# Mamba's product of B with the input on GpSimd in place of VectorE, under a newly searched plan

## What is computed

```
xn = layernorm(x)
x  = x + mamba(xn) + experts(xn)          # L0: Mamba (256 channels, 16 states) and a top-1 mixture of 8 experts
xn = layernorm(x)
x  = x + attention(xn) + local_layers(xn) # L1: 16 heads of 8 with a distance kernel; two local-attention layers, window 64

# inside mamba, for each channel d, state n and token t:
deltaA  = exp(dt * A)                     # dt = softplus(...)
deltaBx = dt * B[t, n] * xs[t, d]
h       = deltaA * h + deltaBx            # a scan over the tokens
y[t, d] = sum over n of h * C[t, n]
```

## Time and profile before

| what | value |
| --- | --- |
| time, median of 3 runs | 2417.98 us (2406.57 to 2421.41) |
| span of the profiled execution | 2423.0 us |
| PE busy | 1912.3 us, 79% |
| DVE busy | 1905.3 us, 79% |
| ACT busy | 1819.8 us, 75% |
| POOL busy | 611.8 us, 25% |
| DMA, mean | 52 GB/s |
| chain that ended last | PE 29%, DVE 29%, issue 20%, ACT 18% |

### The profile page before, as it was taken

How to read it: one execution, slowest core, us unless ns; L and a number is a source line. 1 busy time by engine, 2 the same in 40 slices (tenths; PEclk the granted TensorE clock), 3 DMA queues, 4 the chain that set the end, 5 groups by cost and what they waited for, 6 DMA issues and landing times.

```text
span 2423.0 us, 31144 instructions
## 1 busy us (share of the span) xinstructions
PE 1912.3 (79%) x10610; PEld 1286.1 (53%) x10610; DVE 1905.3 (79%) x2685; ACT 1819.8 (75%) x2507; POOL 611.8 (25%) x270
## 2 busy tenths in 40 slices
PE   3767788898777888887787888878778787888776
PEld 2533446675545555554555555545445555556555
DVE  5878885538998799869997998878986988765563
ACT  2435778888768888787778887788778687888884
POOL 2532211222222213212232222322222222213220
PEclk9887879998879789888888888989898988997887
DMA  7731205531110120011101110101101110000000
GB/s 242 240 106 58 70 18 146 148 88 62 44 44 9 49 75 27 9 50 53 48 5 41 40 56 18 45 11 47 40 23 41 42 55 18 1 1 5 1 1 5
DMA packets 67517, 126.19 MB, mean 52 GB/s; under 512 B 8836, under 2 KB 40132, under 8 KB 67236
## 3 DMA queue, kind: packets, MB, share of 16 engines
q1 hardware_dynamic: 61808, 113.19, 14.7%
q0 software_dynamic: 2816, 7.21, 0.9%
q10 hardware_dynamic: 2740, 3.80, 0.4%
HBM read 111.33 MB, written 12.85 MB: 51 GB/s over the span
## 4 chain that ended last, share of the span: by engine, by line
PE 29%; DVE 29%; issue 20%; ACT 18%; DMA 2%; SPq 1%; DVEq 0%; ACTq 0%; another core or an unknown queue 0%
PE ps L776 6%; DVE hB L1458 6%; PE ps L968 5%; DVE hB L1464 3%; PE ps L1010 3%; DVE hB L1452 3%; PE ps L1070 3%; ACT L771 3%; ACT arena L1281 2%; ACT arena L1289 2%; DVE arena L1529 2%; DVE n_c L1537 2%; DVE lss L1583 2%; ACT arena L1355 2%; DVE rb L1590 2%
## 5 line engine op out<-in xcount | busy, mean ns | idle before, releaser
L1749 POOL TENSOR_TENSOR arena<-arena 128x1024 f32<-128x1024 f32 x128 | 359.2, 2826 | 972.5 <-ACT arena L1283 972.5
L776 PE MATMUL ps<-w_ident,arena 128*128 128x128 f32 x1647 | 276.6, 316 | 135.6 <-ACT arena L1355 42.8
L968 PE MATMUL ps<-hB,w_ident 128*128 128x512 f32 x512 | 305.6, 728 | 70.7 <-DVE hB L1464 68.8
L776 PEld LDWEIGHTS ps<-w_ident,arena 128*128 128x128 f32 x1647 | 223.8, 164 | 228.3 <-issue 113.6
L1458 DVE TENSOR_TENSOR_SCAN hB<-dA,hB 128x1024 f32<-128x1024 f32 x128 | 321.1, 2514 | 1.0 <-ACT dA L1245 0.6
L1753 POOL TENSOR_TENSOR arena<-arena,rb 128x1024 f32<-128x1024 f32 x64 | 159.2, 2487 | 622.5 <-DVE rb L1590 622.5
L1070 PE MATMUL ps<-w_l_wqkv,arena 128*128 128x512 f32 x384 | 205.3, 666 | 30.7 <-DVE rb L1590 12.5
L1245 ACT ACTIVATE dA<-mv,w_A_log 128x510 f32<-128x510 f32 x256 | 168.3, 714 | 70.9 <-DVE hB L1458 68.0
L1452 DVE TENSOR_TENSOR hB<-BC,mv 128x1024 f32<-128x1024 f32 x128 | 194.3, 1522 | 29.8 <-PE ps L968 28.1
L1529 DVE TENSOR_SCALAR arena<-ps 128x1024 f32<-128x1024 f32 x128 | 155.8, 1217 | 58.9 <-PE ps L1010 54.6
L1355 ACT ACTIVATE arena<-ps,nmx 128x128 f32<-128x128 f32 (+1 forms) x512 | 159.2, 394 | 55.6 <-DVE nmx L1610 52.7
(11 more groups left out here) (210 smaller groups left out, 4066.0 us busy)
## 6 DMA issues: line engine op xcount, KB each, us to landing
BC<-bc_d SPq DMA_DIRECT2D x128, 512.0 KB
BC<-in_experts SPq DMA_DIRECT2D x16, 514.0 KB
arena<-in_experts SPq DMA_DIRECT2D x15, 514.0 KB
mv<-in_experts SPq DMA_DIRECT2D x15, 514.0 KB, 3.4
arena<-in_x SPq DMA_DIRECT2D x8, 256.0 KB, 5.5
xnT_d<-arena SPq DMA_DIRECT2D x8, 256.0 KB, 10.9
hB<-xnT_d SPq DMA_DIRECT2D x8, 256.0 KB
x<-in_x SPq DMA_DIRECT2D x8, 256.0 KB, 2.8
```

What stands on the lines that cost most here:

```text
L776: return t.transpose(out_, in_, ident[0:k, 0:k])
L968: e = t.matmul(lb(), ident, hB[k % 2][:, j], start=q == 0 and j == 0, stop=q == NQ - 1 and j == NG - 1)
L1749: g.tensor_tensor(la[m % 2][:, half], la[m % 2][:, half], cl[:, half], ALU.subtract).then_inc(g_sub, 1)
```

## The change

`m_bx` moves from the vector program to the GpSimd program, with the same waits (the buffer's `m_sum` of two steps before, `du`, the load of B); whoever waited for `v_bx` (the scan, SP's next load of B) now waits for `g_bx`. All the planner's numbers are replaced: costs in `STAGES`, a landing time for each engine in `LANDS`, and `LATER` and `STREAM`, which were searched anew. The planner also has a new rule: units named in `DUAL` (on DVE) and in `POOLED` (on POOL) don't run at the same time in the plan, the later one waits for the earlier to end. The order on every engine changes with this.

```
 STAGES = {
-    ... "m_bx": [("DVE", 1.35)], "m_scan": [("DVE", 2.4)], "m_hc": [("DVE", 1.35)], "m_sum": [("PE", 2.3)],
+    ... "m_bx": [("POOL", 2.36)], "m_scan": [("DVE", 2.28)], "m_hc": [("DVE", 1.22)], "m_sum": [("PE", 1.72)],
...
-LANDS = {"SP": 4.5, "POOL": 2.0}
+LANDS = {"PE": 0.27, "ACT": 0.12, "DVE": 0.12, "SP": 4.5, "POOL": 0.15}
+DUAL = ("m_du", "m_scan", "m_hc", "m_fin", "qn", "g_hd")
+POOLED = ("g_sub", "qkv", "m_bx")
-LATER = {"down": 7, "e_down": 10, "e_lg": -58, ...
+LATER = {"down": -23, "e_down": 12, "e_lg": -121, ...
...
+                if e == "DVE" and unit[0] in DUAL:
+                    takes += max(0.0, pool_until - now)
+                    dual_until = now + takes
+                if e == "POOL" and unit[0] in POOLED:
+                    takes += max(0.0, dual_until - now)
+                    pool_until = now + takes
...
 vector_program:
-                elif u == "m_bx":
-                    ...
-                    v.tensor_tensor(hB[k % 2], Bb[q % 2], bc(du[:, c:c + 1], [P, NG, T]), ALU.mult).then_inc(v_bx, 1)
                 elif u == "m_scan":
-                    v.wait_ge(v_bx, m + 1)
+                    v.wait_ge(g_bx, m + 1)
 gpsimd_program:
+                elif u == "m_bx":
+                    q, c = divmod(k, CH)
+                    m = STEPS * i + k
+                    if m >= 2:
+                        g.wait_ge(p_ys, m - 1)
+                    if k < 2:
+                        g.wait_ge(v_du, CH * (i + 1))
+                        g.wait_ge(p_xp, 3 * (i + 1))
+                        g.wait_ge(d_bc, 16 * (i + 1))
+                    g.wait_ge(d_B[q % 2], 16 * ((NQ * i + q) // 2 + 1))
+                    g.tensor_tensor(hB[k % 2], Bb[q % 2], bc(du[:, c:c + 1], [P, NG, T]), ALU.mult).then_inc(g_bx, 1)
 sync_program, m_B:
-                        s.wait_ge(v_bx, CH * (m - 1))
+                        s.wait_ge(g_bx, CH * (m - 1))
```

More of the change, by code:

```diff
@@ L64 @@
[L64 to L72, removed]
-    "shift": [("PE", 0.4), ("ACT", 0.8)], "norm": [("DVE", 0.2), ("ACT", 0.5)], "qn": [("DVE", 1.25)], "heads": [("PE", 1.2), ("ACT", 0.9)],
@@ new lines @@
+    "m_ex": [("ACT", 1.34)], "m_bx": [("POOL", 2.36)], "m_scan": [("DVE", 2.28)], "m_hc": [("DVE", 1.22)], "m_sum": [("PE", 1.72)],
+    "m_fin": [("DVE", 1.47)], "x_load": [("SP", 0.1)], "m_out": [("PE", 1.8), ("DVE", 0.69)],
+    "f_yg": [("POOL", 4.8)], "f_ln": [("DVE", 2.46), ("ACT", 0.55)], "f_xn": [("DVE", 1.11)], "f_tr": [("PE", 0.44), ("DVE", 0.68)],
+    "g_qkv": [("PE", 0.65), ("DVE", 0.62)], "g_sq": [("ACT", 1.06), ("DVE", 1.54)], "g_norm": [("ACT", 0.9)],
+    "g_hd": [("DVE", 0.29), ("PE", 0.44), ("ACT", 0.59)], "g_score": [("PE", 1.06), ("DVE", 1.22)], "g_ln": [("ACT", 4.05)],
@@ L112, in stages, with lands @@
     if u == "m_in":
-        return [("PE", 1.1), ("ACT", 0.6)] if k % 2 else [("PE", 1.1), ("DVE", 2.9), ("ACT", 0.65)]
+        return [("PE", 0.86), ("ACT", 0.62)] if k % 2 else [("PE", 0.86), ("DVE", 3.15), ("ACT", 0.62)]
     if u == "e_scat":
-        return [("POOL", 1.3 * TT * (GP[n + 1] - GP[n]))]
+        return [("POOL", 1.5 * TT * (GP[n + 1] - GP[n]))]
     if u == "qkv":
-        return [("PE", 1.15), ("ACT", 0.5)] if k % 3 else [("PE", 2.3), ("ACT", 0.95), ("DVE", 3.55), ("POOL", 2.4)]
+        return [("PE", 0.86), ("ACT", 0.6)] if k % 3 else [("PE", 1.72), ("ACT", 1.02), ("DVE", 3.6), ("POOL", 2.36)]
     return STAGES[u]
+def lands(unit, engine):
+    return 2.0 if engine == "POOL" and unit[0] in ("e_scat", "f_yg") else LANDS[engine]
 def stream(unit):
@@ L454, in schedule @@
                 if best[2] and best[2] != table:
[L455 removed]
+                    takes += LOAD_TIME * (2 if best[2] == "tan" and table == "ln" else 1)
                     table = best[2]
+                if e == "DVE" and unit[0] in DUAL:
[4 more added lines that the diff above has]
+                    pool_until = now + takes
                 free_at[e] = now + takes
@@ L459, in schedule @@
                 line(unit, e).pop(0)
-                lands = LANDS.get(e, 0.0) if e == "SP" or unit[0] in ("e_scat", "f_yg") else 0.15
-                events.append((now + takes + lands, done, unit, stage))
+                events.append((now + takes + lands(unit, e), done, unit, stage))
                 done += 1
```

59 lines of the change are left out of this document (27 added, 32 removed), and 13 rows, old and new, of the table STREAM.

## The result

The changed kernel takes 2472.60 us (median of 4 runs, 2469.73 to 2481.34) against 2419.69 of the kernel before (4 runs, 2406.57 to 2427.78): a measured ratio of 1.0242, 95% interval [1.0204, 1.0280] (the two medians alone give 1.0219, inside it). It is slower by 2.4%; I had forecast 2358, 2.5% faster, with 2455 as the upper end. The profiled execution has a span of 2480.0 us, 57 more than before; it is the slowest of its four runs, so spans overstate the difference a little.

A forecast was written before the change was run, and what follows sets the result against it. No engine bounds it alone; DVE leads from 600 to 2080 us (86.7%), PE and ACT close behind. Terms -65 - 10 + 40 - 5 - 20 = -60 on the 2423.0 span give 2363, less 5 for the median: 2358; range 2265 to 2455.

The forecast's parts named there:

- +40: First stretch: pair 0's Mamba ends 40 us later, near 208 us, its sixth product waiting for the scatter in POOL's queue.
- 12.3 us for two steps: Pair 0 after the scatter: two products, two scans, one product with C and `m_sum` take 12.3 us, 68 for eleven steps.
- -65: 600 to 2080 us: DVE falls from 1283.8 to 1192 us of work, making the stretch 65 us shorter.
- -10: 170 to 380 us, where DVE leads: it loses 24.0 us, gets 10 back in turns; 10 us gained.
- -5: ACT's list: 138 table loads in place of 146, 10 us less, of which half may count.
- -20: Whole kernel: an order planned with true durations leaves fewer accidental waits, 20 us gained, with ends -60 and +20.
- The turns eat it: Rival, chance 0.17: DVE and POOL excluding each other costs DVE 2.0 us per product, giving 2487 us.
- Hidden: Rival, chance 0.20: PE and ACT get no faster, only DVE's waits grow; nothing gained in 170-380 and 600-2080, 2433 us.

The follow-up runs named there:

- b_moved: Kernel before, its order kept on every engine, with all 128 products moved from DVE's list to POOL's at their planned times; 2503.94 us, ratio 1.0382.
- all_dve: Changed kernel's order with all 128 products back on DVE, each directly before its scan; 2531.11 us, 1.0489 of the kernel before.
- b_half: Order of the kernel before, pair 0's products on DVE, 112 on POOL with half of each left out; 2392.27 us, 0.9869 of the kernel before.
- a_half: Changed kernel with half of each POOL product left out (one of two states) from the third on; 2429.56 us, 1.0077 of the kernel before.
- a_memset: Changed kernel with each POOL product replaced by three fills of its output tile, reading no SBUF; 2442.27 us, 1.0094 of the kernel before.
- s_mix: Pair 0's products on DVE, 112 on POOL, order searched anew with corrected planner costs; 2417.41 us, 0.9982 of the kernel before.
- s_mix2: Pair 0's products on DVE, 112 on POOL, order searched with corrected costs from the other starting point; 2389.37 us, 0.9866 of the kernel before.
- s_pool: All products on POOL, order searched anew with corrected planner costs; 2491.93 us, 1.0293 of the kernel before.
- s_pool2: All products on POOL, order searched with corrected costs from the due times of the kernel before; 2463.00 us, 1.0187 of that kernel.
- s_dve: All products on DVE, order searched with corrected costs from the due times of the changed kernel; 2377.11 us, 0.9832 of the kernel before.
- s_dve2: All products on DVE, order searched with corrected costs from the due times of the kernel before; 2375.48 us, 0.9817 of that kernel.

## Why the prediction was wrong

**The +40 of the first stretch was 64.** The mechanism that I named exists, and alone, in the old order, it is worth 27 of 37 us (b_moved). But the step added up a chain through POOL and took for granted that DVE would be ready at its end. The rows of the new order on DVE had to be read beside it: ten expert additions stand ahead of the sixth scan and wait 36 us for PE, and with all products on DVE the start is still 223. The planner had more than half of this in it: by its own clock pair 0's last result comes at 196.4 us in the new plan and at 158.9 in the old one. My 12.3 us for two steps was also short by 1.9: `m_sum` was taken at 1.78 us, while two of them take 6.2 to 6.5 in a stretch in which PE is granted 0.66. That the total came within 24 us of mine is in part luck: the 24 transfers on which I built the sum cost nothing here.

**The -65 and -10 failed at the conversion.** The account of DVE was near the mark. The turns rose by 49 us over 128 products, 0.38 each on the two lines; all that DVE does besides the product rose by 95 us (1905.3 - 194.3 to 1805.9), 0.74 each, where 0.6 were forecast. The product's median is 2.368 us for 2.36. DVE's share in the middle is 82.6% for "near 82", but by luck: DVE has 1234 us of work there for 1192, in a longer stretch. What failed is "if the three keep the sum of shares that they have (2.457)", which gave 1443 us, and with it the -65 (1415): with DVE lighter the sum fell to 2.421, and the stretch took 1495 us. The shares of PE and ACT stayed as they were (80.2 to 80.3%, 78.8 to 79.3%), and DVE alone emptied. From 170 to 380 the -10 became +30; from pair 0's last result to pair 1's it takes 208 us before, 211 in b_moved, 239 in the changed kernel and 245 in all_dve, so that this belongs to the order and not to the product's place.

Why DVE's relief buys no time stays open in part. The turns that came with the product account for 30 to 51 us. I suspected the chain `m_sum`, product, scan, product with C, which became longer by 1.15 us a step (2.36 for 1.22), plus a handover each way; the waits fit (64.0 us of the scan for POOL, 392.3 of POOL for PE's `m_sum`), and so does b_half in the old order. But in the order of the changed kernel a_half made the product 1.09 us shorter and gained no more in the rest than its turns, so there the length alone isn't the limit. What remains is the order: with the products on DVE this order's rest is 2306 for 2255, though it was made without them there.

**The price of the turns.** I charged them to DVE's busy time and then divided by a sum of shares or by a share, 0.41 to 1.15 us of time for 1 of DVE's. a_memset gives 0.4 to 1.2, so it doesn't tell the two rules apart. Even so, free of the product's turns, the rest would have gained 58 us by the profiles and 41 by the medians, not the 100 of -65, -10, -5 and -20 that already had turns in it.

**The -20 for the new order as such** was a term that couldn't be had. The order without the move is 4.9% slower (all_dve): 55 us at the start and 51 in the rest. The move in the old order is 3.8% slower (b_moved). The new plan ended at 2357.1 us on the planner's clock, the old at 2377.6: 20.5 less, my very term, though the two clocks use different costs; on the chip they are 2480.0 and 2423.0. One search's draw weighs up to half as much as the whole change: the two starts for the same placement differ by 28 us in s_mix and s_mix2, by 29 in s_pool and s_pool2, by 2 in s_dve and s_dve2.

**The -5 for table loads**: 138 loads, as read; what they bring can't be seen.

**The rivals.** "The turns eat it", to which I gave 0.17, has the nearest number, 2487 for 2472.6, but not by its mechanism: it asked for 2.0 us of DVE per product, at least 1.58, and found 0.74. "Hidden", at 0.20, is nearest in kind: little in the stretches behind the start. Its own number was 2433; only with 64 put for 40, and without the -20 and -5, does it give a span of 2423 + 64 = 2487, 7 above the measured one, and the stretches come to nothing only as a sum (+30, -25, +15, -28). None of the rivals had the new order itself as a loss.

**What I put at nothing**, the rest of POOL's queue, held: ACT waits 0.6 us in all for the subtractions of line 1774, in one place.

The Trainium skill (GPSIMD Engine Reference, "Engine selection") advises against this move. I had set it aside because POOL isn't full; the runs bear it out in all three orders that were searched for it (1.0242, 1.0293 and 1.0187 of the kernel before). The Trainium skill (SBUF — State Buffer, "Who interferes with whom") also restricts the exclusion to GpSimd instructions that read SBUF, and a_memset shows just this, below.

## What to carry to other kernels

Moving work off an engine that waits as often as it works need not buy any time: don't divide its lighter load by a share. Write down the chain that the work stands in before and after, on the lists of both engines, with what stands ahead of each link; that would have shown the additions on DVE and the 55 us of the new order. On GpSimd the move has two prices that its free time doesn't show. Whatever stands in its queue (24 indirect transfers, 32 to 34 us) stands ahead of the product, and costs as much of this as nothing else covers: 27 us in the old order, nothing in the new one. And each instruction that reads SBUF holds up VectorE's with two SBUF inputs; undoing this was worth 0.4 to 1.2 us of time for 1 us of VectorE's. Where an order is searched, compare placements only with an order searched for each: the product on DVE is then 3.6 to 4.9% faster than on GpSimd, with up to 29 us of chance between two searches.
